# Order of loads, early offsets and one product for two sums ahead of the first tile of a two-layer graph kernel

## The chip, the cores and the metric

One core of a Trainium2 chip. The time is device microseconds of one execution, the median of several. Lower is better.

## The reference

Input `x` is 4096 x 128, `adj` a 4096 x 4096 matrix of zeros and ones. Layer 0 computes, with h = x W:

```
e     = leaky_relu((h @ a_src)[:, None] + (h @ a_dst)[None, :], 0.2)
valid = (adj > 0) & (h.sum(axis=1) != 0)[None, :]
att   = softmax(where(valid, e, -1e9)), zeroed where not valid or below 1e-4, times the row's number of valid edges
x     = layernorm(x + elu(h + att @ h))
```

Layer 1 takes scores = leaky_relu(x @ ks.T, 0.2), sets those without an edge to -9e15, and computes x = layernorm(x + softmax(scores) @ ks).

## The kernel before

The rows are cut into 32 tiles of 128. A tile's 128 x 4096 attention lies in SBUF with the row on the partition. For each tile, layer 0 adds a mask (one 128 x 4096 bf16 tile of adjacency, loaded by a DMA that GpSimd issues with a cast from int32) to the destination scores `d_all`, takes the row maximum, bends (leaky relu), raises to exp with the row's offset as bias, cuts small entries, transposes on TensorE in four chunks of 1024 columns (`turn0`), copies these to SBUF and multiplies with h (`sum0`). Layer 1 does the like with the keys. Each engine has its own queue, written out by hand; engines meet only through semaphores. In a slot `t` TensorE works on tile t in layer 0 and on tile t - 1 in layer 1.

PSUM holds `work`, three slots of two banks (1024 f32 columns each), used in turn by everything that is transposed or scored, and two more banks for sums.

The change lies ahead of slot 1. There the program does, in this order:

- SP loads x in four parts, then the keys (`k_first`, `k_rest`), then the first two x tiles. GpSimd loads adjacency tile 0 when x part 1 has landed, tile 1 when part 3 has, then the f16 keys (`k_parts`).
- TensorE transposes x (`turn_x`) into `xT`; two vectors from W and a give v_src, v_dst and v_one (W times ones). `make_d(c)` multiplies 512 columns of `xT` with v_one and with v_dst, each widened to 128 equal columns: bank 0 of a `work` slot then holds the row sums of h, bank 1 the destination scores, both repeated on all 128 partitions. It is done 8 times. `make_h(r)` computes h in six fills of `work`.
- ScalarE reads them: `find_sign(c)` writes the sign of the sums to `zero_cols` (bf16), `keep_d(c)` copies the scores to `d_all`. Among them stand `first_bend0(k)`, the leaky relu of quarter k of tile 0, and `keep_h`. Then `raise0(0, 0)` and `raise0(0, 1)`, exp of the two halves.
- VectorE builds mask 0 (`build_mask(0)`), then per quarter `zero_quarter` (sign 0 becomes a large negative number), the minimum with the mask (line 720) and the addition of `d_all` with its row maximum (line 724). `build_mask(1)` stands between quarters 1 and 2. After quarter 3 the four maxima are reduced to `top0` (line 768, it raises `masked0`), then the whole of tile 1 is masked (lines 619, 627), then `threshold0(0)` and `cut(0, 0)`, `cut(0, 1)` wait for the exps. `first_slot` follows: mask 2, `keep_k_low` (the rest of the f16 keys, line 752), minimum 2, the reduction `absent` (line 780, from which GpSimd counts edges), maximum 2, `residual0(0)` (line 646, it waits for `sum0` and for GpSimd's `coef0`), then the low parts of the keys `k_low_part(c)`.
- GpSimd computes the row offset of tiles 0 and 1 in three dependent 128x1 instructions (`offset0`: neg line 866, row 870, bias 873), and issues the loads of tiles 2 and 3 behind them, then `coefficient(0)` (lines 879 to 891: edges, z_sum, rz, gate, coef).
- TensorE goes on with `turn0(0, c)`, three chunks of `sum0`, `turn_k(0)`, `turn_k(1)`, the last chunk of `sum0`, `turn_k(2)`, `turn_k(3)` (its `work` slot waits for `k_low_part(0)`), `turn_q(0)` and the scores of tile 0 (`score`, lines 313 to 318). With score chunk 3 begins slot 1.

Of the kernel before, what the change touches and what calls it, by code (L numbers as in the profile page):

```python
# [5 lines left out]
P = 128  # L6
# [22 lines left out]
def graph_layers(nc, x, adj, W, a, ks, out):  # L29
# [5 lines left out]
    PER = CHUNK // P  # L35
    D_CHUNKS = N // BANK
    HALF = N // 2
# [8 lines left out]
    with ExitStack() as ctx:  # L46
# [42 lines left out]
        v_sb = sb("v_sb", [P, 3])  # L89
        v_dst_wide = sb("v_dst_wide", [P, P])  # L90
        v_one_wide = sb("v_one_wide", [P, P])
        first_s = sb("first_s", [P, 2])
# [62 lines left out]
        xT_ready, h_ready, kT_high, kT_low = sem("xT_ready"), sem("h_ready"), sem("kT_high"), sem("kT_low")  # L155
        sign_found, zero_found, d_ready, first_masked = sem("sign_found"), sem("zero_found"), sem("d_ready"), sem("first_masked")
        first_topped, first_bent, first_counted = sem("first_topped"), sem("first_bent"), sem("first_counted")
# [36 lines left out]

        X_AT, D_AT, H_AT = 0, CHUNKS, CHUNKS + D_CHUNKS
        H_PER = 6
# [7 lines left out]
        @block.sync  # L204
        def _(sp):
            x_blocks = x.rearrange("(b p) d -> p b d", p=P)
            for c in range(CHUNKS):
                part = slice(c * PER, (c + 1) * PER)
                sp.dma_start(x_all[:, part, :], x_blocks[:, part, :]).then_inc(xall_in[c], 16)
            k_blocks = ks.rearrange("(b p) d -> p b d", p=P)  # L210
            sp.dma_start(k_first, k_blocks[:, 0:SPLIT * PER, :]).then_inc(kall_in, 16)
            sp.dma_start(k_rest[:, :, 0:D], k_blocks[:, SPLIT * PER:BLOCKS, :]).then_inc(kall_in, 16)
            sp.dma_start(x_sb[0][:, :], x_rows[0]).then_inc(x_in[0], 16)
            sp.dma_start(x_sb[1][:, :], x_rows[1]).then_inc(x_in[1], 16)

            def slot(t):
                if t + 2 < TILES:
                    sp.wait_ge(low0_ready, t + 1)
                    sp.dma_start(x_sb[t % 2][:, :], x_rows[t + 2]).then_inc(x_in[t % 2], 16)
                if t >= 2:  # L220
                    w = t - 2
                    sp.wait_ge(x2_ready, w + 1)
                    sp.dma_start(out_rows[w], x2[w % 2][:, :]).then_inc(out_sent[w % 2], 16)

            for t in range(TILES + 2):
                slot(t)
            for p in range(2):
                sp.wait_ge(out_sent[p], 16 * (TILES // 2))

        @block.tensor  # L230
        def _(pe):
# [11 lines left out]
            def make_d(c):  # L243
                pe.wait_ge(xT_ready, c + 2 if c < 3 else CHUNKS)
                if c >= 3:
                    pe.wait_ge(d_ready, c - 2)
                    pe.wait_ge(sign_found, c - 2)
                rhs = xT[:, c * BANK:(c + 1) * BANK]
                place = (D_AT + c) % SLOTS
                pe.matmul(work[:, place, 0:BANK], v_one_wide[:, :], rhs, start=True, stop=True)  # L250
                pe.matmul(work[:, place, BANK:CHUNK], v_dst_wide[:, :], rhs, start=True, stop=True).then_inc(d_made, 1)

            def make_h(r):
                if r < 3:
                    pe.wait_ge(d_ready, r + 6)
                    pe.wait_ge(sign_found, r + 6)
                else:
                    pe.wait_ge(h_ready, r - 2)
# [6 lines left out]

            def turn_k(c):
                if c < 3:
# [20 lines left out]
            pe.wait_ge(wide_ready, 2)  # L288
            for c in range(D_CHUNKS):
                make_d(c)  # L290
            for r in range(H_FILLS):
                make_h(r)
            pe.wait_ge(kall_in, 32)

# [26 lines left out]
            def turn0(t, c):  # L321
# [3 lines left out]
                elif t > 0:  # L325
                    pe.wait_ge(bent1, 4 * (t - 1) + c + 2)
                else:
                    pe.wait_ge(h_ready, (5, 6, 4)[c])
                turn((1, 2, 0, 1)[c], c, lambda b: att0[t % 2][:, b * P:(b + 1) * P]).then_inc(turned0, 1)
# [97 lines left out]
        def _(act):  # L427
# [3 lines left out]
            for c in range(CHUNKS):  # L431
                act.wait_ge(x_turned, c + 1)
                nc.scalar.copy(xT[:, cols(c)], work[:, (X_AT + c) % SLOTS, :]).then_inc(xT_ready, 1)
            def find_sign(c):
                act.wait_ge(d_made, c + 1)
                nc.scalar.activation(zero_cols[:, c * BANK:(c + 1) * BANK], work[:, (D_AT + c) % SLOTS, 0:BANK],
                                     ACT.Sign).then_inc(sign_found, 1)

            def keep_d(c):
                act.wait_ge(d_made, c + 1)  # L440
                nc.scalar.copy(d_all[:, c * BANK:(c + 1) * BANK],
                               work[:, (D_AT + c) % SLOTS, BANK:CHUNK]).then_inc(d_ready, 1)

# [85 lines left out]
            def to_first_slot():  # L529
                find_sign(0)  # L530
                keep_d(0)
                find_sign(1)
                keep_d(1)
                find_sign(2)
                keep_d(2)
                find_sign(3)
                keep_d(3)
                first_bend0(0)
                find_sign(4)
                keep_d(4)  # L540
                find_sign(5)
                keep_d(5)
                first_bend0(1)
                find_sign(6)
                keep_d(6)
                find_sign(7)
                keep_d(7)
                keep_h(0)
# [60 lines left out]
        def _(dve):  # L609
# [106 lines left out]
            def first_mask0(k):  # L716
                both = adj_sb[0]
                dve.wait_ge(mask_built, 1)
                dve.wait_ge(zero_found, k + 1)
# [3 lines left out]
                dve.wait_ge(d_ready, (k + 1) * D_CHUNKS // QUARTERS)  # L723
# [4 lines left out]
            def zero_quarter(k):  # L728
                dve.wait_ge(sign_found, (k + 1) * D_CHUNKS // QUARTERS)
                z = zero_cols[:, quarter(k)]  # L730
                nc.vector.tensor_scalar(z, z, 0.0, -NO_EDGE, ALU.is_equal, ALU.mult).then_inc(zero_found, 1)

# [12 lines left out]
            dve.wait_ge(consts_ready, 2)  # L745
            nc.vector.tensor_scalar(v_dst_wide[:, :], ones[:, :], v_sb[:, 1:2], None, ALU.mult).then_inc(wide_ready, 1)
            nc.vector.tensor_scalar(v_one_wide[:, :], ones[:, :], v_sb[:, 2:3], None, ALU.mult).then_inc(wide_ready, 1)

# [5 lines left out]
            def to_first_slot():  # L754
                build_mask(0)
                zero_quarter(0)
                first_mask0(0)
                zero_quarter(1)
                dve.wait_ge(s_made, 1)
                nc.vector.tensor_copy(first_s[:, :], s_ps).then_inc(first_s_ready, 1)  # L760
                first_mask0(1)
                build_mask(1)
                zero_quarter(2)
                first_mask0(2)
                zero_quarter(3)
                first_mask0(3)
                dve.wait_ge(first_topped, QUARTERS)
                nc.vector.tensor_reduce(top0[0][:, :], first_top[:, :], AX.X, ALU.max).then_inc(masked0, 1)
                zero_mask(1)
                mask0(1)  # L770
                threshold0(0)
                cut(0, 0)
                cut(0, 1)

            def first_slot():
                build_mask(2)
                keep_k_low()
                zero_mask(2)
                dve.wait_ge(first_bent, QUARTERS)
                nc.vector.tensor_reduce(absent[0][:, :], first_absent[:, :], AX.X, ALU.add).then_inc(first_counted, 1)  # L780
                mask0(2)
# [60 lines left out]
        def _(pool):  # L842
# [16 lines left out]
            def offset0(f):  # L859
                p = f % 2  # L860
                pool.wait_ge(masked0, f + 1)
                if f < 2:
                    pool.wait_ge(first_s_ready, 1)
                else:
                    pool.wait_ge(s_ready, H_FILLS)
                nc.gpsimd.tensor_scalar(neg0[p][:, :], top0[p][:, :], -1.0, s_of(f), ALU.mult,  # L866
# [35 lines left out]
            def deviation1(w):  # L902
# [47 lines left out]
```

## Time and profile before

| what | value |
|---|---|
| median of 3 runs | 885.51 us (885.41 to 885.6) |
| the profiled execution: its time | 886.26 us |
| its span | 884.4 us |
| busy: PE, DVE, ACT, POOL | 849.4, 783.3, 763.8, 231.0 us |
| chain that ended last, by engine | PE 90%, DVE 3%, DMA 2%, POOL 2%, issue 2%, ACT 1% |
| PE busy, first four fortieths of the span (22 us each) | 7, 4, 7, 9 tenths |

### The profile page before, as it was taken

To read this page: it belongs to the slowest core of one execution; us is meant where nothing else is said; L and a number is where in the kernel's file an instruction comes from. 1 tells how busy PE (TensorE), PEld (TensorE's weight loads), DVE (VectorE), ACT (ScalarE), POOL (GpSimd) and SP (SyncE) were. 2 spreads that over 40 slices of the span, in tenths; PEclk is the share of its full clock that TensorE was granted. 3 is DMA by queue.
4 is the path that set the end of the run, shared out by engine and by line. 5 is a ranking of instruction groups with operands and counts; after the bars stand their busy time and mean duration, and the time that the engine had idled before them with its cause. 6 is when DMAs were issued, how large, how long until landed. Compare 5 with 4: busy or idle time off the path is not lost.

```text
span 884.4 us, 17581 instructions
## 1 busy us (share of the span) xinstructions
PE 849.4 (96%) x7111; PEld 732.9 (83%) x7111; DVE 783.3 (89%) x955; ACT 763.8 (86%) x747; POOL 231.0 (26%) x428
## 2 busy tenths in 40 slices
PE   7479999999999999999999999999999999999995
PEld 4376788899888888988888889888888998888885
DVE  1789999999999999999999999999999999998744
ACT  4588988889998888899988888999888889998753
POOL 1431143321223333212233331122333312222200
PEclk9898999999999999999999999999999999999999
DMA  9832222122222211222222112222221122200000
GB/s 236 124 67 50 52 49 41 28 43 55 54 55 54 55 34 30 47 54 55 54 54 54 28 32 53 54 55 54 55 52 24 34 55 54 55 7 7 4 4 10
DMA packets 23408, 43.93 MB, mean 50 GB/s; under 512 B 5024, under 2 KB 18464, under 8 KB 19232
## 3 DMA queue, kind: packets, MB, share of 16 engines
q0 software_dynamic: 7696, 34.34, 21.5%
q1 hardware_dynamic: 15200, 8.39, 3.7%
q8 instruction: 57, 0.93, 0.4%
q14 instruction: 23, 0.19, 0.1%
q10 hardware_dynamic: 432, 0.07, 0.1%
HBM read 75.04 MB, written 2.10 MB: 87 GB/s over the span
## 4 chain that ended last, share of the span: by engine, by line
PE 90%; DVE 3%; DMA 2%; POOL 2%; issue 2%; ACT 1%; POOLq 0%; SPq 0%; DVEq 0%; ACTq 0%
PE bank L336 25%; PE work L234 24%; PE bank L364 10%; PE bank L368 6%; PE work L313 6%; PE work L318 6%; PE work L314 6%; PE bank L365 5%; DMA adj_sb<-adj 1%; DMA att<-x 1%; POOL row L870 0%; POOL edges L879 0%; PE bank L374 0%; DVE att1T L690 0%; ACT att L460 0%
## 5 line engine op out<-in xcount | busy, mean ns | idle before, releaser
L234 PE MATMUL work<-ident,att 128*128 128x128 f32 x2080 | 245.9, 274 | 11.9 <-DMA att<-x 6.0
L234 PEld LDWEIGHTS work<-ident,att 128*128 128x128 f32 x2080 | 232.5, 141 | 19.3 <-issue 9.2
L336 PE MATMUL bank<-h_all,att0T 128*128 128x128 f32 x2048 | 239.1, 275 | 0.0
L336 PEld LDWEIGHTS bank<-h_all,att0T 128*128 128x128 f32 x2048 | 233.7, 192 | 0.0
L500 ACT ACTIVATE att1T<-work 128x1024 f16<-128x1024 f32 (+1 forms) x128 | 125.5, 1048 | 34.7 <-PE work L234 34.7
L640 DVE SCALAR_TENSOR_TENSOR att<-att,cut 128x2048 f32<-128x2048 f32 x64 | 149.7, 2343 | 0.0
L679 DVE CUSTOM_DVE_ANT_0 att<-att,mask 128x2048 f32<-128x2048 f32 x64 | 144.3, 2290 | 5.4 <-ACT att L483 5.4
L364 PE MATMUL bank<-k_parts,att1T 128*128 128x257 f16 x768 | 140.1, 275 | 0.8 <-DVE att1T L690 0.8
L627 DVE CUSTOM_DVE_ANT_0 att<-adj_sb,d_all 128x4096 f32<-128x4096 bf16 x31 | 137.2, 4425 | 1.0
L470 ACT ACTIVATE att<-att,bias 128x2048 f32<-128x2048 f32 x64 | 129.3, 2020 | 7.7 <-POOL bias L873 7.7
L365 PE MATMUL bank<-k_parts,att1T 128*128 128x129 f16 x768 | 134.9, 219 | 0.0
L488 ACT ACTIVATE att<-att,bias 128x2048 f32<-128x2048 f32 x64 | 131.9, 2062 | 2.7 <-DVE bias L685 2.7
L477 ACT COPY att0T<-work 128x1024 f32<-128x1024 f32 x128 | 129.4, 1049 | 1.5 <-PE work L234 1.5
L483 ACT ACTIVATE att<-work 128x1024 f32<-128x1024 f32 x128 | 121.6, 1027 | 8.8 <-PE work L318 8.8
L866 POOL TENSOR_SCALAR neg<-top,s_all 128x1 f32<-128x1 f32 x30 | 9.4, 314 | 425.6 <-DVE top L627 425.5
L690 DVE SCALAR_TENSOR_TENSOR att1T<-work,att1T 128x1024 f16<-128x1024 f32 x96 | 113.9, 1215 | 3.2 <-ACT att1T L500 3.2
L453 ACT ACTIVATE att<-att,s_all 128x4096 f32<-128x4096 f32 x30 | 111.4, 3712 | 0.0
L313 PE MATMUL work<-kT,qT 128*128 128x512 f16 x256 | 97.9, 383 | 0.9 <-ACT qT L510 0.9
L314 PE MATMUL work<-kT,qT 128*128 128x512 f16 x256 | 97.9, 383 | 0.0
L364 PEld LDWEIGHTS bank<-k_parts,att1T 128*128 128x128 f16 x768 | 74.2, 97 | 12.1 <-DVE att1T L690 1.0
L318 PE MATMUL work<-kT,qT 128*128 128x512 f16 x256 | 77.1, 383 | 0.0
L365 PEld LDWEIGHTS bank<-k_parts,att1T 128*128 128x128 f16 x768 | 75.8, 99 | 0.8
(98 smaller groups left out, 836.7 us busy)
## 6 DMA issues: line engine op xcount, KB each, us to landing
adj_sb<-adj POOLq DMA_DIRECT2D x32, 1024.0 KB, 8.6
att<-x SPq DMA_DIRECT2D x4, 512.0 KB, 6.6
x_sb<-x SPq DMA_DIRECT2D x32, 64.0 KB, 8.2
out<-x SPq DMA_DIRECT2D x32, 64.0 KB, 1.6
k_parts<-ks POOLq DMA_DIRECT2D x1, 768.0 KB, 20.6
k_rest<-ks SPq DMA_DIRECT2D x1, 512.0 KB, 21.9
w_sb<-W ACTq DMA_DIRECT2D x1, 64.0 KB, 2.9
a_sb<-a ACTq DMA_DIRECT2D x2, 0.5 KB, 4.8
```

What stands on the lines that cost most here:

```text
L234: mm = pe.transpose(work[:, n % SLOTS, b * P:(b + 1) * P], source(c * PER + b), ident[:, :])
L313: pe.matmul(o, qT[:, 0, :], kT[:, 0, part], start=True, stop=False)
L314: pe.matmul(o, qT[:, 0, :], kT[:, 1, part], start=False, stop=False)
L318: mm = pe.matmul(o, qT[:, 1, :], kT[:, 0, part], start=False, stop=True)
L336: mm = pe.matmul(acc0, att0T[:, k * P:(k + 1) * P], h_all[:, k, :], start=(k == 0), stop=(k == BLOCKS - 1))
L364: pe.matmul(acc1, high1T[:, part], k_parts[:, k, :], start=(k == 0), stop=False)
L365: mm = pe.matmul(acc1[:, D:], low1T[:, part], k_parts[:, k, D:], start=False, stop=(k == BLOCKS - 1))
L477: nc.scalar.copy(att0T[:, cols(c)], work[:, (1, 2, 0, 1)[c], :]).then_inc(copied0, 1)
L488: nc.scalar.activation(att1[:, half(k)], att1[:, half(k)], ACT.Exp, bias=bias1[u % 2][:, :]).then_inc(exp1, 1)
L627: nc.vector.tensor_tensor_reduce(att0[p][:, :], adj_sb[p][:, :], d_all[:, :], 1.0, -NO_ROW_MAX, ALU.add, ALU.max, top0[p][:, :]).then_inc( ...
L640: nc.vector.scalar_tensor_tensor(b, b, cut0[p][:, :], b, ALU.is_ge, ALU.mult).then_inc(cut_done, 1)
L679: nc.vector.tensor_tensor_reduce(att1[:, half(k)], att1[:, half(k)], mask[u % MASKS][:, half(k)], 1.0, -3.0e38, ALU.add, ALU.max, top1[u % ...
```

## The change

Loads: SP waits for adjacency tile 0 ahead of the key loads, GpSimd for tile 1 ahead of its own, and TensorE waits for the keys in `turn_k`.

Destination scores and zero sums: one widened matrix `v_wide` holds v_dst in columns 0 to 63 and v_one in columns 64 to 127, so one product gives the scores on partitions 0 to 63 and the sums on partitions 64 to 127. It is taken over 1024 columns at a time, four times. `keep_d(c)` copies the lower 64 partitions of PSUM twice, to either half of `d_all`. The sums of the second bank go through ScalarE's sign as before, but to each half by an instruction; those of the first bank are tested against zero by VectorE straight from PSUM, to each half by an instruction (`first_zero`). `second_zero` does for 512 columns what `zero_quarter` did for 1024.

Offsets: those of tiles 0 and 1 are computed on VectorE (`first_offset0`). `build_mask(1)` moves behind the offset of tile 0, and the `absent` reduction to a place ahead of the first threshold.

```diff
@@ sync
+            sp.wait_ge(adj_in[0], 16)
             sp.dma_start(k_first, k_blocks[:, 0:SPLIT * PER, :]).then_inc(kall_in, 16)
@@ tensor
             def make_d(c):
                 pe.wait_ge(xT_ready, c + 2 if c < 3 else CHUNKS)
-                if c >= 3:
-                    pe.wait_ge(d_ready, c - 2)
-                    pe.wait_ge(sign_found, c - 2)
-                rhs = xT[:, c * BANK:(c + 1) * BANK]
-                place = (D_AT + c) % SLOTS
-                pe.matmul(work[:, place, 0:BANK], v_one_wide[:, :], rhs, start=True, stop=True)
-                pe.matmul(work[:, place, BANK:CHUNK], v_dst_wide[:, :], rhs, start=True, stop=True).then_inc(d_made, 1)
+                if c == 3:
+                    pe.wait_ge(d_ready, 2)
+                    pe.wait_ge(sign_found, 2)
+                    pe.wait_ge(first_zero_found, 2)
+                for b in range(CHUNK // BANK):
+                    mm = pe.matmul(work[:, (D_AT + c) % SLOTS, b * BANK:(b + 1) * BANK], v_wide[:, :],
+                                   xT[:, c * CHUNK + b * BANK:c * CHUNK + (b + 1) * BANK], start=True, stop=True)
+                mm.then_inc(d_made, 1)
...
-                    pe.wait_ge(h_ready, (5, 6, 4)[c])
+                    pe.wait_ge(h_ready, (6, 4, 5)[c])
@@ scalar
             def keep_d(c):
                 act.wait_ge(d_made, c + 1)
-                nc.scalar.copy(d_all[:, c * BANK:(c + 1) * BANK],
-                               work[:, (D_AT + c) % SLOTS, BANK:CHUNK]).then_inc(d_ready, 1)
+                source = work[0:HP, (D_AT + c) % SLOTS, :]
+                nc.scalar.copy(d_all[0:HP, cols(c)], source).then_inc(d_ready, 1)
+                nc.scalar.copy(d_all[HP:P, cols(c)], source).then_inc(d_ready, 1)
+
+            def find_sign(c):
+
+                act.wait_ge(d_made, c + 1)
+                source = work[HP:P, (D_AT + c) % SLOTS, BANK:CHUNK]
+                for lower in range(0, P, HP):
+                    nc.scalar.activation(zero_cols[lower:lower + HP, c * CHUNK + BANK:(c + 1) * CHUNK], source,
+                                         ACT.Sign).then_inc(sign_found, 1)
...
                 find_sign(1)
                 keep_d(1)
+                first_bend0(0)
                 find_sign(2)
                 keep_d(2)
+                first_bend0(1)
                 find_sign(3)
                 keep_d(3)
...
                 keep_h(0)
                 first_bend0(2)
                 raise0(0, 0)
@@ vector
+            def first_zero(c):
+                dve.wait_ge(d_made, c + 1)
+                source = work[HP:P, (D_AT + c) % SLOTS, 0:BANK]
+                for lower in range(0, P, HP):
+                    nc.vector.tensor_scalar(zero_cols[lower:lower + HP, c * CHUNK:c * CHUNK + BANK], source, 0.0, -NO_EDGE,
+                                            ALU.is_equal, ALU.mult).then_inc(first_zero_found, 1)
+
+            def second_zero(c):
+                dve.wait_ge(sign_found, 2 * c + 2)
+                z = zero_cols[:, c * CHUNK + BANK:(c + 1) * CHUNK]
+                nc.vector.tensor_scalar(z, z, 0.0, -NO_EDGE, ALU.is_equal, ALU.mult).then_inc(second_zero_found, 1)
...
+            def first_offset0(f):
+                p = f % 2
+                dve.wait_ge(masked0, f + 1)
+                dve.wait_ge(first_s_ready, 1)
+                nc.vector.tensor_scalar(neg0[p][:, :], top0[p][:, :], -1.0, s_of(f), ALU.mult,
+                                        ALU.subtract).then_inc(neg0_ready, 1)
+
+                dve.wait_ge(neg0_ready, f + 1)
+                nc.vector.scalar_tensor_tensor(row0[p][:, :], neg0[p][:, :], NO_ROW_MAX / 2, neg0[p][:, :], ALU.is_lt,
+                                               ALU.mult).then_inc(row0_ready, 1)
+                dve.wait_ge(row0_ready, f + 1)
+                nc.vector.scalar_tensor_tensor(bias0[p][:, :], row0[p][:, :], SLOPE, row0[p][:, :], ALU.mult,
+                                               ALU.min).then_inc(bias0_ready, 1)
...
             def to_first_slot():
-                build_mask(0)
-                zero_quarter(0)
-                first_mask0(0)
-                zero_quarter(1)
+                first_zero(0)
                 dve.wait_ge(s_made, 1)
                 nc.vector.tensor_copy(first_s[:, :], s_ps).then_inc(first_s_ready, 1)
+                first_zero(1)
+                build_mask(0)
+                second_zero(0)
+                first_mask0(0)
+                first_zero(2)
+                second_zero(1)
                 first_mask0(1)
-                build_mask(1)
-                zero_quarter(2)
+                first_zero(3)
+                second_zero(2)
                 first_mask0(2)
-                zero_quarter(3)
+                second_zero(3)
                 first_mask0(3)
                 dve.wait_ge(first_topped, QUARTERS)
                 nc.vector.tensor_reduce(top0[0][:, :], first_top[:, :], AX.X, ALU.max).then_inc(masked0, 1)
+                first_offset0(0)
+                build_mask(1)
                 zero_mask(1)
                 mask0(1)
+                first_offset0(1)
+                dve.wait_ge(first_bent, QUARTERS)
+                nc.vector.tensor_reduce(absent[0][:, :], first_absent[:, :], AX.X, ALU.add).then_inc(first_counted, 1)
                 threshold0(0)
@@ gpsimd
+            pool.wait_ge(adj_in[1], 16)
             pool.wait_ge(k_one_ready, 2)
             nc.gpsimd.dma_start(k_parts[:, :, D:2 * D],
                                 ks.rearrange("(b p) d -> p b d", p=P)[:, 0:SPLIT * PER, :]).then_inc(k_high, 16)
-            offset0(0)
             load_adj(2)
-            offset0(1)
             load_adj(3)
             coefficient(0)
```

The slots of `make_h` and their waits are renumbered to the four products.

## Rows read from the trace of the kernel before

**Rows 1.** Chain of waits, whole span: start us, us, what.

```profile
101.30 3.49 PE work L234 x32
...
836.82 3.49 PE work L234 x32
```

**Rows 2.** Chain of waits, first 80 us.

```profile
7.87 11.33 DMA adj_sb<-adj
19.23 1.23 DVE mask L614
...
31.98 2.28 POOL neg L866
...
56.83 4.34 POOL edges L879
...
63.10 0.36 DVE y L646
```

**Rows 3.** Timeline, 0 to 45 us: start us, us, instruction, idle time before it.

```profile
14.22 0.60 ACT L436 ACTIVATE zero_cols<-work 128x512 bf16<-128x512 f32 x1 [1.15 <-PE work L251]
...
15.94 0.60 ACT L436 ACTIVATE zero_cols<-work 128x512 bf16<-128x512 f32 x1 [0.64 <-PE work L251]
...
31.77 2.28 DVE L619 TENSOR_TENSOR adj_sb<-mask,zero_cols 128x4096 bf16<-128x4096 bf16 x1
...
34.09 4.42 DVE L627 CUSTOM_DVE_ANT_0 att<-adj_sb,d_all 128x4096 f32<-128x4096 bf16 x1
```

**Rows 4.** All instructions of line 870: ns least, median, most; first and last start.

```profile
L870 POOL TENSOR_SCALAR row<-neg x32: 310/311/4337, 34.4 to 798.5; 128x1 f32<-128x1 f32 x32
```

**Rows 5.** Adjacency tile, first 110 us: from issue to landing.

```profile
DMA to landing us min/median/max: 8.5/10.0/13.7
```

**Rows 6.** Groups by shape, first 80 us: count, busy us, mean ns, idle us before.

```profile
L724 DVE CUSTOM_DVE_ANT_0 att<-adj_sb,d_all 128x1024 f32<-128x1024 bf16 x4 | 4.9, 1225 | 0.1
L735 DVE TENSOR_TENSOR kT<-work,kT 128x1024 f16<-128x1024 f32 x4 | 4.8, 1208 | 0.0
L436 ACT ACTIVATE zero_cols<-work 128x512 bf16<-128x512 f32 x8 | 4.8, 603 | 3.1 <-PE work L251 3.1
...
L433 ACT COPY att<-work 128x1024 f32<-128x1024 f32 x4 | 4.1, 1013 | 5.6 <-PE work L234 5.6
...
L720 DVE TENSOR_TENSOR adj_sb<-mask,zero_cols 128x1024 bf16<-128x1024 bf16 x4 | 2.8, 692 | 0.3
L731 DVE TENSOR_SCALAR zero_cols<-zero_cols 128x1024 bf16<-128x1024 bf16 x4 | 1.7, 422 | 0.4 <-ACT zero_cols L436 0.4
...
L633 DVE TENSOR_SCALAR cut<-z 128x1 f32<-128x1 f32 x2 | 0.4, 210 | 6.7 <-ACT att L470 6.7
```

**Rows 7.** Timeline, 43 to 69 us.

```profile
43.22 2.09 PE L262 MATMUL work<-w_sb,att 128*128 128x129 f32 x8 [10.24 <-ACT h_all L523]
...
45.44 4.62 DVE L640 SCALAR_TENSOR_TENSOR att<-att,cut 128x2048 f32<-128x2048 f32 x2
...
47.89 1.94 PE L234 MATMUL work<-ident,att 128*128 128x128 f32 x16 [0.85 <-DVE att L640]
...
59.02 1.95 PE L336 MATMUL bank<-h_all,att0T 128*128 128x128 f32 x16
...
60.89 0.99 ACT L527 CAST kT<-work 128x1024 f16<-128x1024 f32 x1
...
68.83 0.58 PE L313 MATMUL work<-kT,qT 128*128 128x512 f16 x1 [0.90 <-ACT qT L510]
```

**Rows 8.** Stretches of 1 us: busy time by engine, granted clock, DMA share, GB/s.

```profile
46.00:47.00 1.00, 1.00 (x5) 0.85 (x4) 1.00 (x1) 1.00 (x3) 0.00 (x0) 0.62 0.91 188
67.00:68.00 1.00, 0.48 (x1) 0.18 (x1) 1.00 (x3) 0.20 (x2) 0.73 (x4) 0.62 0.00 0
74.00:75.00 1.00, 1.00 (x6) 0.44 (x5) 0.38 (x1) 0.86 (x1) 0.00 (x0) 0.97 1.17 246
175.00:176.00 1.00, 1.00 (x7) 0.46 (x5) 1.00 (x1) 1.00 (x2) 0.00 (x0) 1.00 1.04 156
```

More of the change, by code:

```diff
@@ L35, in graph_layers @@
     PER = CHUNK // P
-    D_CHUNKS = N // BANK
+    HP = P // 2
     HALF = N // 2
@@ L89, in graph_layers @@
         v_sb = sb("v_sb", [P, 3])
-        v_dst_wide = sb("v_dst_wide", [P, P])
-        v_one_wide = sb("v_one_wide", [P, P])
+        v_wide = sb("v_wide", [P, P])
         first_s = sb("first_s", [P, 2])
@@ L155, in graph_layers @@
         xT_ready, h_ready, kT_high, kT_low = sem("xT_ready"), sem("h_ready"), sem("kT_high"), sem("kT_low")
-        sign_found, zero_found, d_ready, first_masked = sem("sign_found"), sem("zero_found"), sem("d_ready"), sem("first_masked")
+        sign_found, first_zero_found, second_zero_found, d_ready, first_masked = (
+            sem("sign_found"), sem("first_zero_found"), sem("second_zero_found"), sem("d_ready"), sem("first_masked"))
         first_topped, first_bent, first_counted = sem("first_topped"), sem("first_bent"), sem("first_counted")
@@ L191, in quarter @@
             return slice(k * QUARTER, (k + 1) * QUARTER)
-        X_AT, D_AT, H_AT = 0, CHUNKS, CHUNKS + D_CHUNKS
+        X_AT, D_AT, H_AT = 0, CHUNKS, 2 * CHUNKS
         H_PER = 6
@@ L244, in make_d @@
                 pe.wait_ge(xT_ready, c + 2 if c < 3 else CHUNKS)
-                if c >= 3:
-                    pe.wait_ge(d_ready, c - 2)
-                    pe.wait_ge(sign_found, c - 2)
-                rhs = xT[:, c * BANK:(c + 1) * BANK]
-                place = (D_AT + c) % SLOTS
-                pe.matmul(work[:, place, 0:BANK], v_one_wide[:, :], rhs, start=True, stop=True)
-                pe.matmul(work[:, place, BANK:CHUNK], v_dst_wide[:, :], rhs, start=True, stop=True).then_inc(d_made, 1)
+                if c == 3:
[6 more added lines that the diff above has]
+                mm.then_inc(d_made, 1)
             def make_h(r):
                 if r < 3:
-                    pe.wait_ge(d_ready, r + 6)
-                    pe.wait_ge(sign_found, r + 6)
+                    pe.wait_ge(d_ready, 2 * r + 4)
+                    pe.wait_ge(sign_found, 2 * r + 4)
+                    pe.wait_ge(first_zero_found, 2 * r + 4)
                 else:
@@ L266, in turn_k @@
             def turn_k(c):
+                pe.wait_ge(kall_in, 32)
                 if c < 3:
@@ L288, in _ @@
             pe.wait_ge(wide_ready, 2)
-            for c in range(D_CHUNKS):
+            for c in range(CHUNKS):
                 make_d(c)
@@ L292, in _ @@
                 make_h(r)
-            pe.wait_ge(kall_in, 32)
             def score(t, c):
@@ L433, in _, with keep_d @@
                 nc.scalar.copy(xT[:, cols(c)], work[:, (X_AT + c) % SLOTS, :]).then_inc(xT_ready, 1)
+            def keep_d(c):
+                act.wait_ge(d_made, c + 1)
+                source = work[0:HP, (D_AT + c) % SLOTS, :]
+                nc.scalar.copy(d_all[0:HP, cols(c)], source).then_inc(d_ready, 1)
+                nc.scalar.copy(d_all[HP:P, cols(c)], source).then_inc(d_ready, 1)
             def find_sign(c):
                 act.wait_ge(d_made, c + 1)
[L436 to L440, printed above, removed]
-                nc.scalar.copy(d_all[:, c * BANK:(c + 1) * BANK],
-                               work[:, (D_AT + c) % SLOTS, BANK:CHUNK]).then_inc(d_ready, 1)
+                source = work[HP:P, (D_AT + c) % SLOTS, BANK:CHUNK]
+                for lower in range(0, P, HP):
+                    nc.scalar.activation(zero_cols[lower:lower + HP, c * CHUNK + BANK:(c + 1) * CHUNK], source,
+                                         ACT.Sign).then_inc(sign_found, 1)
             def bend0(f):
@@ L533, in to_first_slot @@
                 keep_d(1)
+                first_bend0(0)
                 find_sign(2)
                 keep_d(2)
+                first_bend0(1)
                 find_sign(3)
                 keep_d(3)
[L538 to L547, printed above, removed]
                 keep_h(0)
@@ L718, in first_mask0 @@
                 dve.wait_ge(mask_built, 1)
-                dve.wait_ge(zero_found, k + 1)
+                dve.wait_ge(first_zero_found, 2 * k + 2)
+                dve.wait_ge(second_zero_found, k + 1)
                 nc.vector.tensor_tensor(both[:, quarter(k)], mask[0][:, quarter(k)], zero_cols[:, quarter(k)],
@@ L722, in first_mask0 @@
                 dve.wait_ge(first_masked, k + 1)
-                dve.wait_ge(d_ready, (k + 1) * D_CHUNKS // QUARTERS)
+                dve.wait_ge(d_ready, 2 * k + 2)
                 nc.vector.tensor_tensor_reduce(att0[0][:, quarter(k)], both[:, quarter(k)], d_all[:, quarter(k)],
@@ L726, in first_mask0 @@
                                                first_top[:, k:k + 1]).then_inc(first_topped, 1)
[L728 to L731, printed above, removed]
+            def first_zero(c):
[8 more added lines that the diff above has]
+                nc.vector.tensor_scalar(z, z, 0.0, -NO_EDGE, ALU.is_equal, ALU.mult).then_inc(second_zero_found, 1)
             def k_low_part(c):
@@ L745, in _ @@
             dve.wait_ge(consts_ready, 2)
-            nc.vector.tensor_scalar(v_dst_wide[:, :], ones[:, :], v_sb[:, 1:2], None, ALU.mult).then_inc(wide_ready, 1)
-            nc.vector.tensor_scalar(v_one_wide[:, :], ones[:, :], v_sb[:, 2:3], None, ALU.mult).then_inc(wide_ready, 1)
+            nc.vector.tensor_scalar(v_wide[:, 0:HP], ones[:, 0:HP], v_sb[:, 1:2], None, ALU.mult).then_inc(wide_ready, 1)
+            nc.vector.tensor_scalar(v_wide[:, HP:P], ones[:, HP:P], v_sb[:, 2:3], None, ALU.mult).then_inc(wide_ready, 1)
+            def first_offset0(f):
[10 more added lines that the diff above has]
+                                               ALU.min).then_inc(bias0_ready, 1)
             def keep_k_low():
@@ L778, in first_slot @@
                 zero_mask(2)
-                dve.wait_ge(first_bent, QUARTERS)
-                nc.vector.tensor_reduce(absent[0][:, :], first_absent[:, :], AX.X, ALU.add).then_inc(first_counted, 1)
                 mask0(2)
@@ L861, in offset0 @@
                 pool.wait_ge(masked0, f + 1)
[L862 to L865, printed above, removed]
+                pool.wait_ge(s_ready, H_FILLS)
                 nc.gpsimd.tensor_scalar(neg0[p][:, :], top0[p][:, :], -1.0, s_of(f), ALU.mult,
```

## The prediction

> **What bounds the kernel now.** I read the chain of waits first. From the first full slot to the last but one the same entry (32 transposes) returns from 101.30 to 836.82 us, 29 slots of 25.36 us, always on TensorE [rows 1]. The diff changes no instruction of these slots but two branches of a helper, so what it can move is the start of slot 1, before which the chain runs over other engines [rows 2]: the landing of adjacency tile 0 (19.2 us), the mask work on VectorE, GpSimd's offset (31.98 to 39.1), its edge count (56.83) and the residual it holds up (63.10). The timeline then says what stood beside each. GpSimd's `row` took 4.34 us once and 0.31 in its other 31 runs, and that once it lies inside VectorE's 4.42 us mask instruction, `neg` inside the 2.28 us one before it [rows 2 to 4]. The edge count, 4.34 us too, starts 0.1 us behind the same 4.42 us instruction of tile 2. So some 6 us of the offset and 4 of the edge count are a wait for VectorE, not work.
>
> **Keys behind the adjacency.** SP now issues the two key loads when tile 0 has landed, GpSimd its own behind tile 1. `x_sb` follows the keys on SP. GpSimd's load 2 no longer stands behind offset 0: issued at 30.3 (below), it lands 8.5 to 10 later, by 40, and is read at 44.65. Tile 0 took 11.33 us; the shortest landing of an adjacency tile is 8.5 [rows 2, 5]. It still shares with the last two x loads, so I take 16.4 to 18.4 us, middle 17.4 instead of 19.2. Keys and tile 1 must land by 45.8 and 30.9 (below). Before, all this traffic was over by 32 us, and its bytes are the same. I cost it at nothing.
>
> **One product per 1024 columns.** TensorE did 16 products of 512 columns, now 8. Product c of the new kernel occupies the time of one old pair: ready at 14.2, 15.9, 17.7, 19.4 the first two are 1.72 apart [rows 3]. The readers change. ScalarE did 2 signs and 2 copies of 512 per 1024 columns, at a pitch of 0.48 each (the next starts before one of 0.60 has ended), 1.9 us; now 2 signs of 512 and 2 copies of 1024 on 64 partitions. The trace has no 64-partition form. The bounds are half of the 128-partition copy (1.01 for 1024 columns [rows 6]) and twice it; I take it whole, pitch 0.93. That is 2.8 us per 1024 columns, 3.7 more in all. VectorE gets 8 reads of 64x512 from PSUM: bounds 0.42 (the 1024-column SBUF form) and 1.21 (1024 columns with a PSUM operand), I take half the latter, 0.60, so 1.2 per 1024 columns; its remaining zero pass halves (0.42 to about 0.3, pitch with the semaphore 0.4) [rows 6].
>
> The new front, by queue. VectorE: `first_zero(0)` 14.2 to 15.4, scores copy, `first_zero(1)` 15.95 to 17.15; mask 0 at 17.4, 1.15; then 0.4 + 0.72 + 1.15 per quarter (zero, minimum, maximum) and 1.2 for each `first_zero`: quarter 0 done 20.8, quarter 1 at 24.3, quarter 2 at 27.7. ScalarE: sign(0), keep(0), sign(1), keep(1) to 19.9; waits for quarter 0; bend 20.9 to 22.0; sign(2), keep(2) to 24.8; bend, sign(3), keep(3) to 28.7. The last maximum waits for that keep: 28.8 to 30.0. So the two engines bind about equally, tile 0's 0.25 us included, and the row maximum is ready at 30.2, before at 31.86: 1.7 earlier.
>
> **Offset on VectorE.** Three 128x1 instructions, 0.21 each by the `cut` threshold's row [rows 6], with semaphores 0.25: 0.75 in all (bounds 0.3 and 1.1). The bias is ready at 30.95 instead of 39.1. ScalarE: exp half 0 from 31.0, bend(3), `keep_h(1)`, exp half 1 done at 36.9, before 45.1 (the threshold, 0.21, stands between it and the cut at 45.44): 8.2 earlier. But VectorE is late next. Mask 1 was built ahead of quarter 2, where VectorE waited for signs; now it stands behind the offset: 1.15, then minimum and maximum of tile 1 (6.75, from 31.77 to 38.5 [rows 3]), offset 1 (0.75) and the moved `absent` reduction (0.2): the threshold can't start before 39.8, `cut` at 40.05, before at 45.44 [rows 7]. Gain at this point 5.4, not 8.2; 1.9 of it is build and offset that lost their cover.
>
> **TensorE's clock takes some back.** Before, h fills ran from 43.2 on right ahead of the transposes at 47.89; the engine had idled 10.2 us, the granted clock was 0.5 (1.2 GHz) and rose at about 46.8 (0.62 is the mean of that microsecond) [rows 7, 8]. Now the fills end at 38.6 and the transposes start at 42.45 behind idle time, so at 1.2 GHz. It rose 3.5 us after work began there and 5.2 after the scores began (68.83 to 74.1) [rows 7, 8]. Transposes at half speed for 3.5 to 5.2 us lose 1.75 to 2.6, less the 0.45 that TensorE waited for the second cut anyway; taken 1.7. The four transposed chunks and the sum then end at 60.97 - 5.4 + 1.7 = 57.2 [rows 7].
>
> **Edge count moved forward.** It starts at 39.8 beside the cuts. If each of its five GpSimd instructions waits for one VectorE instruction it is done at 51.4 (cuts, mask 2, key part, minimum 2), before 57.2: nothing on the path. VectorE: cuts to 44.65, mask 2, key part, minimum, maximum of tile 2 as before, ending at 61.1 (where the blocked edge count came free [rows 2]) - 5.4 - 0.1 = 55.6. So the residual waits for TensorE at 57.3 in place of GpSimd at 63.10 [rows 2]: 5.8 earlier. The first key copy on ScalarE stands behind the transposed copies, 60.89 - 5.4 + 1.7 = 57.2, done 58.1, and doesn't hold that up by more than 0.1. From there to the scores all is as before, 68.83 - 5.75 = 63.1. Offset 2 stays on GpSimd behind mask 2 and coefficient 0, both done.
>
> The scores ran at 1.2 GHz for 5.2 us before, losing 2.6; the clock had fallen at 67.2, in a stretch (61 to 68.8) with little work [rows 8]. With the 2 us wait for GpSimd gone this stretch is 2 us shorter. Either the same again (0) or no fall (+2.6, of which VectorE's masks let through about 1.8); I add 0.6. **Sum: 5.75 + 0.6 = 6.35 us off the profiled execution**, 886.26 (span 884.4 and 1.86 around it) to 879.9. The median of runs is 0.75 below the profiled one, so 879.2.
>
> **Rivals.**
> (a) Clock kept through the scores: 1.8 instead of 0.6 and a loss of 0.8 instead of 1.7 at 42.45: 5.75 + 0.9 + 1.8 = 8.45, so 877.1. For it: shorter gaps. Against: the clock fell in the same place before.
> (b) Tile 0 lands no sooner, 19.2: the front moves 1.8 us later, gain 4.5: 881.0. For it: x loads still share; against: 2 MB of keys leave its way.
> (c) Adjacency tile 2 is held up: its issue is now followed by back-to-back VectorE work to 38.6, and GpSimd stood still beside such work [rows 3, 4]. Held to 38.6 it lands at 47.1 to 48.6 instead of 40, mask 2 waits from 44.65, maximum 2 ends at 58.1 to 59.6, 0.9 to 2.4 behind TensorE: about 880.8. Against: in the slot of 174 us a load was moving at 175 with VectorE busy throughout [rows 8]. A rule speaks for it: while VectorE runs an instruction in a two-port mode, GpSimd cannot write the descriptors of a DMA that it issues (the Trainium skill, "SBUF — State Buffer", section "SBUF: two separate sides"). By its wording only the mask build here is of that kind, which makes the landing 1.2 later and the sum no different, 879.2; if it held for all of VectorE's forms in the stretch, it would be the 880.8 above. The row at 175 agrees with the narrow reading.
> (d) Slower: 64-partition instructions (8 copies, 8 signs, 8 PSUM reads) that read one half and write the other cost double. ScalarE's front grows by 4 x (1.86 + 0.96) = 11.3 us, of which about 1 falls into its waits. The cut then starts 10.3 later: 885.5 - 6.3 + 10.3 = 889.5. It decides at an extra of about 60% an instruction, where the gain is gone. For it: no row of the form. Against: full-width rows go by columns.
> (e) The offset on VectorE brings nothing because mask 1 moved behind it: the cut at 45.4. Against: the sum above leaves VectorE no such length. What is left is the edge count's 2.0 less the clock's part: about 884.5.
>
> **Chances.** Forecast 0.50 (own range 878 to 880.5), (a) 0.20, (b) 0.12, (c) 0.08, (d) 0.06, (e) 0.04. The range 876.5 to 883.5 leaves out (d), (e) and the tails of the rest, under 0.2: its low end is (a) with half-width copies somewhat under 1 us, its high end (b) and (c) together and 0.9 more for dearer half-width forms. Within 0.2% is 1.8 us, about what can be told from no change here. Faster by more: all but (d) and (e), 0.90; within: (e), 0.04; slower: (d), 0.06.
>
> **What would show it.** Tile 0's mask starts near 17.4. The first two `row` and `neg` are VectorE's, near 30.5. Exp half 1 ends near 37 and the cut starts near 40, with VectorE and not ScalarE as the last. Transposes from 42.4 at a granted 0.5. The residual at 57.3, released by TensorE. Scores from 63.1. Slots still 25.36 apart, 101.30 now near 95. Wrong: a 64-partition copy far from 1.0 us; a cut after 42; a residual still released by GpSimd; slots of another length.

## The result and the profile after

The changed kernel takes 882.15 us (median of 5, 880.22 to 882.62), the kernel before 885.51 in the same session; the ratio is 0.9956, 95% interval 0.9941 to 0.9971. It is faster by 3.9 us with 2.6 to 5.2 as the interval (3.4 by the medians), where 6.3 was forecast. Two of its five runs took 880.2 and 880.5 us and three 882.2 to 882.6; its profiled execution is the longest of them, 882.62 us with a span of 880.7. In one experiment below, `e6_offset_pool`, one run of eleven took 1113.8 us at a mean granted clock of 0.749 (0.981 to 0.989 in the others) and is left out of its numbers.

The chain of waits of the changed kernel, against [rows 1]:

```profile
97.57 3.49 PE work L238 x32
...
833.07 3.49 PE work L238 x32
```

Again 29 slots of 25.36 us, all 3.73 earlier. So the whole gain stands ahead of slot 1, as forecast. Its timeline there, in order of time (start us, us, instruction, idle time before it and what ended it):

```profile
14.45 1.21 ACT L451 ACTIVATE zero_cols<-work 64x512 bf16<-64x512 f32 x2 [1.15 <-PE work L254]
14.45 1.42 DVE L735 TENSOR_SCALAR zero_cols<-work 64x512 bf16<-64x512 f32 x2 [4.28 <-PE work L254]
15.68 1.00 ACT L443 COPY d_all<-work 64x1024 f32<-64x1024 f32 x1
...
16.71 1.00 ACT L444 COPY d_all<-work 64x1024 f32<-64x1024 f32 x1
17.07 0.83 SPq L215 DMA_DIRECT2D att1T<-ks  x1
17.61 1.23 DVE L616 TENSOR_SCALAR mask<-adj_sb 128x4096 bf16<-128x4096 bf16 x1
17.74 1.21 ACT L451 ACTIVATE zero_cols<-work 64x512 bf16<-64x512 f32 x2
...
30.40 1.23 DVE L727 CUSTOM_DVE_ANT_0 att<-adj_sb,d_all 128x1024 f32<-128x1024 bf16 x1 [0.74 <-ACT d_all L444]
...
31.86 0.21 DVE L763 TENSOR_SCALAR neg<-top,first_s 128x1 f32<-128x1 f32 x1
...
32.56 2.01 ACT L480 ACTIVATE att<-att,bias 128x2048 f32<-128x2048 f32 x1 [0.28 <-DVE bias L770]
...
36.43 2.01 ACT L480 ACTIVATE att<-att,bias 128x2048 f32<-128x2048 f32 x1
...
41.34 4.63 DVE L642 SCALAR_TENSOR_TENSOR att<-att,cut 128x2048 f32<-128x2048 f32 x2
...
43.76 6.60 PE L238 MATMUL work<-ident,att 128*128 128x128 f32 x32 [3.66 <-DVE att L642]
...
52.79 4.42 POOL L918 TENSOR_SCALAR coef<-gate,rz 128x1 f32<-128x1 f32 x1
...
59.36 0.35 DVE L648 SCALAR_TENSOR_TENSOR y<-bank,coef,h_all 128x128 f32<-128x128 f32 x1 [2.31 <-PE bank L342]
...
65.23 0.58 PE L319 MATMUL work<-kT,qT 128*128 128x512 f16 x1 [0.90 <-ACT qT L520]
```

What to see in it: SP's wait for tile 0 ends at 17.07, the mask build stands at 17.61 right behind `first_zero(1)` with no wait of its own (19.23 before [rows 2]). The row maximum is reduced at 31.67 (31.70 before), so this front gained nothing, and the offset starts right behind it at 31.86. The bias is there at 32.5 instead of 39.1. VectorE runs on without a wait to the cut at 41.34 (45.44 before), while the exps were done at 38.4. The residual is at 59.36 and waits for TensorE, no longer for GpSimd at 63.10; GpSimd's last instruction for it (`coef`) ended at 57.21. The 32 transposes take 6.6 us; before, the two lots of 16 took 1.94 and 1.97 with a gap of 0.28. The granted clock is the third number from the end of each row below (a row gives the stretch and its length, the busy time of PE, PEld, which is TensorE's loading of weights, DVE, ACT and POOL, then the clock, the DMA share and GB/s):

```profile
42.00:43.00 1.00, 0.00 (x0) 0.00 (x0) 1.00 (x1) 0.00 (x0) 1.00 (x1) 0.94 1.42 131
43.00:44.00 1.00, 0.24 (x1) 0.24 (x2) 1.00 (x2) 0.00 (x0) 0.92 (x2) 0.50 0.71 139
49.00:50.00 1.00, 1.00 (x8) 1.00 (x7) 1.00 (x1) 0.82 (x1) 1.00 (x1) 0.64 0.00 0
63.00:64.00 1.00, 0.14 (x1) 0.14 (x1) 1.00 (x3) 0.63 (x1) 0.81 (x3) 0.68 0.00 0
70.00:71.00 1.00, 1.00 (x6) 0.42 (x5) 0.79 (x1) 0.54 (x1) 0.00 (x0) 0.90 0.99 197
```

The mean of a microsecond tells when the clock changed within it. It fell to 0.50 (1.2 GHz) at 42.9, in 3.7 us of idleness behind the h fills and just ahead of the transposes, and came back at about 49.7; it fell once more at 63.3, ahead of the scores, until 70.2.

### The profile page after: what moved, and what is told of

The parts are those of the page before. It is cut to its first block, busy times and chain, and to the rows that moved or that the text cites. A ratio compares the mean times of both kernels' runs of the same rounds, so it can differ in the third digit from the quotient of the medians.

```text
span 880.7 us, 17559 instructions
## 1 busy us (share of the span) xinstructions
PE 846.5 (96%) x7095; PEld 733.3 (83%) x7095; DVE 789.0 (90%) x969; ACT 768.3 (87%) x747; POOL 231.6 (26%) x422
## 4 chain that ended last, share of the span: by engine, by line
PE 92%; DVE 3%; ACT 2%; issue 2%; DMA 1%; SPq 0%; POOL 0%; POOLq 0%; DVEq 0%; ACTq 0%
PE work L238 25%; PE bank L342 25%; PE bank L370 10%; PE bank L374 6%; PE work L319 6%; PE work L320 6%; PE work L324 6%; PE bank L371 5%; DMA att<-x 1%; PE bank L380 0%; ACT att L463 0%; DVE att1T L692 0%; PE work L254 0%; SPq L212 0%; DVE mask L616 0%
## 5 line engine op out<-in xcount | busy, mean ns | idle before, releaser
L238 PEld LDWEIGHTS work<-ident,att 128*128 128x128 f32 x2080 | 235.0, 143 | 22.3 <-issue 8.6
L370 PEld LDWEIGHTS bank<-k_parts,att1T 128*128 128x128 f16 x768 | 74.2, 97 | 12.0 <-DVE att1T L692 1.0
L918 POOL TENSOR_SCALAR coef<-gate,rz 128x1 f32<-128x1 f32 x32 | 78.0, 2438 | 3.3
```

The source lines that it names most:

```text
L238: mm = pe.transpose(work[:, n % SLOTS, b * P:(b + 1) * P], source(c * PER + b), ident[:, :])
L370: pe.matmul(acc1, high1T[:, part], k_parts[:, k, :], start=(k == 0), stop=False)
```

## Experiments

Each kernel is compared with the kernel before in its own session (885.6 to 886.6); the ratios carry that, the medians differ by up to 1 us between sessions. "Changed" is the changed kernel. The diffs shown here are abridged. The clock's part varies from trace to trace, and there is one trace of each kernel: the 32 transposes took from 4.2 us (before) to 6.6 (changed).

**The product.** `e1_no_product` takes it out of the changed kernel, `e2_product_only` puts it alone into the kernel before.

```diff
@@ e1_no_product, against changed
-pe.matmul(work[:, place, b * BANK:...], v_wide, xT[:, ...])                    # 8
+pe.matmul(work[:, place, 0:BANK], v_one_wide, rhs); pe.matmul(..., v_dst_wide, rhs)  # 16
-first_zero(c), second_zero(c), find_sign(c), keep_d(c)   # half-width, on 1024 columns
+find_sign(c), keep_d(c)   # 128x512, for each of 8 products
+zero_quarter(k)
```

> The changed kernel with the 16 full-width products, 8 signs, 8 copies and zero_quarter of the kernel before in place of the half-width product; loads, VectorE offsets and the earlier edge count stay. Theory P (the half-width forms cost what the saved product work was worth, and more): the row maximum of tile 0 is ready by about 30.3 us instead of 31.8, and the time is 1 to 1.5 below the changed kernel, about 881. Rival (the product brought its share of the 3.4 us): the row maximum comes later than 31.8 and the time is 883.5 or more.

> The kernel before with the half-width product, signs, copies and first_zero alone; keys first, offsets on GpSimd, edge count late, mask 1 between quarters 1 and 2 as before. Theory P: no gain, 885.5 to 887, the row maximum at 31.8 to 33.5. Rival (the product brings a share by itself): 884 or less.

Without the product 878.91 us, ratio 0.9920 (0.9907 to 0.9932), against 0.9956 with it: 3.2 us faster. With the product alone 887.92, ratio 1.0026 (1.0017 to 1.0036): 2.3 us slower than before, and a little above the 885.5 to 887 expected; its row maximum is reduced at 33.96 instead of 31.70. VectorE in `e1_no_product`:

```profile
16.34 1.23 DVE L615 TENSOR_SCALAR mask<-adj_sb 128x4096 bf16<-128x4096 bf16 x1 [6.11 <-DMA adj_sb<-adj]
...
23.21 0.43 DVE L732 TENSOR_SCALAR zero_cols<-zero_cols 128x1024 bf16<-128x1024 bf16 x1 [0.85 <-ACT zero_cols L437]
...
29.17 0.16 DVE L782 TENSOR_REDUCE top<-first_top 128x1 f32<-128x4 f32 x1
...
38.84 4.64 DVE L641 SCALAR_TENSOR_TENSOR att<-att,cut 128x2048 f32<-128x2048 f32 x2
```

The row maximum is ready 2.5 us earlier than with the product (31.67) and so is the cut. VectorE now waits 6.11 us for tile 0 and 0.85 for a sign; with the product it didn't wait for tile 0, and waited 0.74 for ScalarE's last copy. Theory P holds, and by more than the 1 to 1.5 expected. Part of the 3.2 us is the clock's: the 32 transposes took 5.28 us here and 6.60 in the changed kernel.

**What a half-width instruction costs.** `e7_halves` doubles the score copies of the kernel before in two ways (one run, 888.28 us).

```diff
-nc.scalar.copy(d_all[:, ...], source)
+nc.scalar.copy(to[0:64], source[0:64]); nc.scalar.copy(to[64:128], source[64:128])   # c < 4
+nc.scalar.copy(to, source); nc.scalar.copy(unused, source)                           # c >= 4
```

> The kernel before with two ways to copy the destination scores twice: for products 0 to 3 the lower and the upper 64 partitions by an instruction each, partition onto the same partition; for products 4 to 7 all 128 partitions twice, the second time to unused memory. It measures the pitch of ScalarE's instructions. Theory H (64 partitions lose the overlap with the next instruction): pitch of a 64-partition copy of 512 columns 0.58 to 0.62, of a 128-partition one 0.48. Rival (the crossing to the other half costs it): here, where nothing crosses, both have 0.48. Second rival (two reads of the same PSUM columns in a row lose it): both have 0.6. The time says nothing else.

```profile
15.01 0.57 ACT L444 COPY d_all<-work 64x512 f32<-64x512 f32 x1
15.59 0.58 ACT L445 COPY d_all<-work 64x512 f32<-64x512 f32 x1
16.24 0.60 ACT L437 ACTIVATE zero_cols<-work 128x512 bf16<-128x512 f32 x1
...
25.11 0.58 ACT L447 COPY d_all<-work 128x512 f32<-128x512 f32 x1
25.58 0.60 ACT L448 COPY kT<-work 128x512 f32<-128x512 f32 x1
26.06 0.63 ACT L437 ACTIVATE zero_cols<-work 128x512 bf16<-128x512 f32 x1
```

The duration is the same, 0.57 on 64 partitions and 0.58 on 128, but behind a half-width copy the next instruction starts 0.58 us later (15.01 to 15.59), behind a full one 0.47 (25.11 to 25.58, 25.58 to 26.06). Nothing crosses to other partitions here, and the full-width copy read the same columns twice in a row: both rivals fall, theory H holds. In the changed kernel the copies of 1024 are 1.03 apart (15.68, 16.71, 17.74), the signs 0.6.

**The key loads.** `e5_keys_early` undoes them in the changed kernel, `e10_keys_only` does them alone in the kernel before (the three waits on `adj_in` and `kall_in`).

> The changed kernel with the key loads issued as before, ahead of the adjacency. Theory L (the later key loads bring tile 0's mask forward by what lies between its landing and first_zero(1)): tile 0's mask starts at 19.4 to 19.5 instead of 17.6, the row maximum at about 33.5 instead of 31.8, the time 1.5 to 1.9 higher than the changed kernel, about 883.8. Rival (ScalarE's reads bind the front, tile 0's landing is hidden): row maximum within 0.3 of 31.8, 882.1.

> The kernel before with the later key loads alone. Theory L: tile 0's mask starts at 16.4 instead of 19.2, but ScalarE's signs and copies bind the last quarter, so the row maximum is ready at about 30.3 instead of 31.9 and all that follows moves by that: 884, 1.5 below before. Rival: the later keys or the moved f16 load cost something of their own and it is 885.5 or more.

Undone: 882.99 us, ratio 0.9969 (0.9957 to 0.9981), 1.1 by ratio over the changed kernel, whose intervals overlap; in its trace tile 0's mask starts at 19.27 and the row maximum is reduced at 33.33 instead of 31.67. Alone: 883.85, ratio 0.9974 (0.9962 to 0.9985), 2.3 faster than before, with the mask at 16.40 and the maximum at 29.24, 2.5 ahead of before and 1 ahead of what I expected. Theory L holds in the traces and, alone, in the time; undone, the time moved by less than the 1.5 to 1.9 expected, which by itself would show nothing.

**The offset.** `e6_offset_pool` puts the two offsets back on GpSimd; `e11_offset_only` has them on VectorE, with the earlier edge count, as the only edits of the kernel before.

> The changed kernel with the offsets of tiles 0 and 1 back on GpSimd, all else as changed (mask 1 still behind the row maximum, edge count ahead of the threshold). Theory O (GpSimd's three 128x1 instructions wait for VectorE's mask work, one each): neg, row and bias end at about 40.5, exp half 1 at 46.5, the cut at 46.7 instead of 41.3 and later than the kernel before's 45.4, the time 885 to 887. Rival (only part of the wait is real, since the mask 1 build lets neg through): cut below 44, time below 884.

> The kernel before with VectorE's offsets and the earlier edge count alone, mask 1 built between quarters 1 and 2 as before. Theory O: the cut starts at 40.5 instead of 45.4, the residual about 2 us further forward less the low clock's part, time 880.5 to 881.5. Rival (the gain needs the earlier tile 0 too): 883 or more.

`e6_offset_pool`: 885.1 us, ratio 0.9991 (0.9982 to 1.0), 3.1 slower than changed by ratio, with the cut at 45.87 instead of 41.34. All three of GpSimd's 128x1 instructions now take the time of VectorE's instruction beside them:

```profile
31.35 1.22 DVE L616 TENSOR_SCALAR mask<-adj_sb 128x4096 bf16<-128x4096 bf16 x1
31.56 1.20 POOL L894 TENSOR_SCALAR neg<-top,first_s 128x1 f32<-128x1 f32 x1 [8.06 <-DVE top L795]
32.86 2.21 POOL L898 TENSOR_SCALAR row<-neg 128x1 f32<-128x1 f32 x1
35.16 4.37 POOL L901 TENSOR_SCALAR bias<-row 128x1 f32<-128x1 f32 x1
...
40.11 0.31 POOL L894 TENSOR_SCALAR neg<-top,first_s 128x1 f32<-128x1 f32 x1
```

`bias` was the short one in the kernel before; here it stands beside the row-maximum instruction and takes 4.37. So it is the neighbour that makes the time, not the operation. `e11_offset_only`: 879.91 us, ratio 0.9929 (0.9916 to 0.9941), 6.3 faster than before, cut at 39.99; both are somewhat better than expected, and the rival falls. It is by far the largest part of the change, and by itself it is 2.4 us faster than the whole change. No run has the earlier edge count alone, so the 6.3 is of the two together.

**TensorE's clock.** `e3_warm_first` adds 28 transposes into unused PSUM ahead of the first real ones, `e3b_warm_both` another 25 in the gaps ahead of the scores.

```diff
+def idle_work(n):
+    for _ in range(n): pe.transpose(wT_ps, w_sb[:, 0:D], ident[:, :])
+idle_work(28)            # both
 turn0(0, 0) ...
 turn_k(2)
+idle_work(10)            # e3b_warm_both only; 9 behind turn_k(3), 6 behind turn_q(0)
```

> The changed kernel with 28 transposes that nobody reads behind the h fills, ahead of turn0(0, 0). Theory C (the low clock at the first transposes takes 2.4 us back): granted clock 1.00 at 44 us, 32 transposes in about 4.2 us instead of 6.6, time 2 us lower, about 880, and runs closer together. Rival (VectorE's masks of tile 2 end at 57 anyway and bind next): the transposes are faster but the residual starts less than 0.5 us earlier and the time stays 882.

> As e3_warm_first, with 10, 9 and 6 more transposes that nobody reads behind turn_k(2), turn_k(3) and turn_q(0). Theory C: the granted clock stays 1.00 through the first scores, which take 3.9 us instead of 6.5; VectorE's masks then bind in slot 1, and the time is 1 to 2 below e3_warm_first's 879.5, about 878. Rival: VectorE's chain takes it all, 879.5; or the added transposes themselves delay the key transposes and it is above 879.5.

```profile
43.00:44.00 1.00, 0.34 (x3) 0.24 (x3) 1.00 (x2) 0.00 (x0) 0.92 (x2) 1.00 0.80 156
```

`e3_warm_first` (the row above is its own): clock 1.00, the cut and the first transpose at the same 41.35 and 43.76, the 32 transposes in 4.2 us, the residual at 57.25 instead of 59.36, 879.53 us, ratio 0.9931 (0.9919 to 0.9944): 2.2 by ratio, 2.6 by medians; the five runs lie within 1.1 us, those of the changed kernel within 2.4. TensorE's sum was done at 56.89. The residual then waited for GpSimd, whose `coef` took the time of VectorE's row-maximum instruction on tile 2 (done at 57.05):

```profile
52.79 4.42 POOL L923 TENSOR_SCALAR coef<-gate,rz 128x1 f32<-128x1 f32 x1
...
57.25 0.35 DVE L653 SCALAR_TENSOR_TENSOR y<-bank,coef,h_all 128x128 f32<-128x128 f32 x1 [0.19 <-POOL coef L923]
```

`e3b_warm_both`: granted clock 1.00 in every microsecond I read from 60 to 67, 878.12 us, ratio 0.9914 (0.9900 to 0.9927). Both clock losses are real, 2.2 and about 1.4 us, though the intervals of the two kernels overlap a little. In `e3_warm_first` the scores ran at 0.50 for 2.8 us (62.98 to 65.8), not for 5.0 as in the changed kernel; half of 2.8 is the 1.4.

**VectorE's order.** `e4_cut_first` moves tile 1's maximum and offset behind the cuts, the f16 key rest ahead of the threshold, coefficient 0 ahead of load 3.

> The changed kernel with the masks of tile 1's maximum (4.4 us) and its offset moved behind the cuts of tile 0, the f16 key rest (3.3 us) moved ahead of the threshold, and coefficient 0 ahead of load 3 on GpSimd. Theory V (VectorE's tile 1 work holds the cut, not ScalarE's exps): the cut starts at 39.6 instead of 41.3, ScalarE's exp half 1 (38.5) being next, and the time is 1.5 lower, about 880.6. Rival (the residual is bound by VectorE's work in all, which is the same): within 0.5 of 882.1.

879.50 us, ratio 0.9929 (0.9916 to 0.9941): the cut at 39.40, the residual at 56.98 right behind VectorE's mask of tile 2. It gained 2.4 where 1.5 was expected. The idle time ahead of the transposes shrank to 1.88 us and these took 5.24 instead of 6.60: a share of the gain is the clock's.

**All together.** `e8_all` has the full-width products, the order of `e4_cut_first` and 12, 10, 9 and 6 added transposes; `e9_no_product_cut_first` lacks the transposes.

> The full-width products of e1_no_product, the order of e4_cut_first, and transposes that nobody reads in the two gaps (12, then 10, 9 and 6). If the three effects stand beside each other: residual at about 54.6 (VectorE's masks of tile 2 next), scores at 2.4 GHz, time about 876.5. If VectorE already took all: 878.9, as e1_no_product.

> As e8_all without the added transposes. Theory V: the residual moves from 55.5 (e1_no_product) to 54.6, bound by VectorE, so 878 or 0.9 below e1_no_product's 878.9. Rival (TensorE's clock at the first transposes decides again): 878.9 or more.

`e8_all`: 875.92 us, ratio 0.9886 (0.9873 to 0.9900), 6.2 us below the changed kernel by ratio and the fastest of all. Its residual is at 56.40 and not at 54.6: TensorE's sum was done at 54.46, and VectorE's mask of tile 2 ended just at 56.40. Its cut came at 38.93, no earlier than the 38.84 of `e1_no_product`: with this order VectorE reads the f16 keys ahead of the cut, and it waited for them, since their load had been moved behind tile 1. It waited 1.43 us here and 0.84 in `e9_no_product_cut_first`; in the kernel before this load had landed at about 32:

```profile
35.41 3.36 DVE L775 TENSOR_TENSOR k_parts<-att1T,k_parts 128x3072 f16<-128x3072 f32 x1 [1.43 <-DMA k_parts<-ks]
```

So the later key load, which costs nothing in the changed kernel, costs something in this order. `e9_no_product_cut_first`: 878.61 us, ratio 0.9911 (0.9897 to 0.9924), not to be told from `e1_no_product`. Its cut came 0.6 earlier (38.25), its transposes took 6.50 us, and the residual stood at 56.17, behind `e1_no_product`'s 55.5: the rival, with one trace of each.

## Why the prediction was right, and where not

**Direction and place** were right: all of the gain is ahead of slot 1, 101.30 became 97.57, and the slots kept their 25.36 us. The size was 6.35 in the profiled execution, it is 3.64. The 882.15 us lie in the stated range (876.5 to 883.5) but not in the forecast's own (878 to 880.5). That the range held is in part luck: its high end was worked out from rivals (b) and (c), which didn't come, with 0.9 for dearer half-width forms, and what brought the time near that end is those forms and the clock. Three terms of the sum are off.

**The half-width product (row maximum 1.7 earlier: it was 0).** This is the term that failed most. I took a copy of 1024 on 64 partitions at a pitch of 0.93, a sign at 0.48 and a PSUM read at 0.60; they measured 1.03, 0.60 and 0.71. ScalarE needs 3.3 us for 1024 columns instead of 2.8, VectorE 3.75 for a quarter (28.55 - 24.80, from one quarter's end to the next) instead of 3.5. Both queues are full, ScalarE's to the end (VectorE waits 0.74 us for its last copy), so it adds up to 1.4 at the row maximum; 0.2 more is that the products began at 14.45 instead of 14.22. The nearest row was the right duration and the wrong pitch. And I forecast the sum of two edits as one number: the product costs 2.5 us at that place (`e1_no_product`), the key loads bring 2.5 (`e10_keys_only`), so the 1.7 hid a loss. Rival (d) had the sign of this one edit right, with an extra of about 17% on ScalarE (3.3 against 2.8), not 100%.

**The offset and its sequel (the cut 5.4 earlier: 4.1)** were right as a mechanism: GpSimd's 6 us were a wait for VectorE, they went, and VectorE's work on tile 1 was late next. What is missing is the front's loss, 1.6; from the row maximum to the cut the forecast was 9.85 us (30.2 to 40.05) and it took 9.5 (31.83 to 41.34).

**The clock (1.7 lost: 2.4)** was right in place. I didn't follow it through the h fills. It was at 0.50 from 36.1 on, came up at 39.5 during them, and fell again at 42.9, less than 1 us ahead of the transposes. So the transposes ran slow for 6.0 us instead of my 3.5 to 5.2. For the scores I added 0.6 and 0.1 came: they ran at 0.50 for 5.0 us instead of 5.2.

**Edge count and residual** were right in what releases the residual: TensorE's sum, done at 59.25, and not GpSimd. The time of GpSimd's last instruction was not: 51.4 forecast, 57.21 measured. I had given each of the five one VectorE instruction to wait for. The first, `edges`, waited for none (0.19 us). The next two took 2.21 and 3.19 us beside the two cuts and the mask build, `gate` 5.42 beside the f16 key rest and the minimum, and `coef` 4.42 beside the row maximum. So only 2.0 us were left before it would have held the residual again, and in `e3_warm_first` it did.

**Rivals.** (a) is not what happened; `e3b_warm_both` shows what it would have been, 878 (877.1 forecast). (b) did not come: tile 0 had landed by 17.07. (c) did not come: mask 2 was built right behind the cuts, at 45.90. (e) is refuted by the changed kernel itself: mask 1 stands behind the offset there, and the cut is at 41.34, not at 45.4; with the offset back on GpSimd (`e6_offset_pool`) it is at 45.87 and the time 3.1 us higher. `e11_offset_only` says nothing of (e), since it leaves mask 1 where it was. The edits by themselves, as ratios: offset and edge count 6.3 us, key loads 2.3, product -2.3. They don't add up to the 3.9 of the whole, since mask 1 stands behind the offset in the changed kernel and the clock's loss changes. The traces show both: from `e11_offset_only` to the changed kernel the row maximum is reduced at the same time (31.66 and 31.67), but the cut starts 1.35 us later and the transposes take 6.60 us instead of 5.35.

## What to carry to other kernels

Price each edit by itself even where two feed the same event: a gain and a loss of 2.5 us met here in one number near 0. A tiny GpSimd instruction on the critical path took as long here as the VectorE instruction beside it, or as two in a row; put it on the engine that produces its input. Halving TensorE's work in front of two reading engines that are full is worth nothing if it makes them read more often, and a gap that is opened ahead of TensorE can be paid twice, as it was in the changed kernel: once as idle time and once as the clock of the work behind it.

## What the runs showed of the hardware

- ScalarE started the next instruction 0.1 us before a 128-partition copy of 512 columns ended, and not before a 64-partition one ended (pitch 0.47 and 0.58, duration 0.58 and 0.57, in `e7_halves`); whether the copy crosses to the other half makes no difference that the rows show (the next starts 1.03 us behind either of the two copies of 1024 in the changed kernel).
- GpSimd's 128x1 instructions of 0.31 us lasted 1.20, 2.21 and 4.37 us beside VectorE's mask build, minimum and row-maximum instructions (`e6_offset_pool`), and `gate`, 0.32 elsewhere, 5.42 beside two in a row (changed kernel). The Trainium skill ("GPSIMD Engine Reference", section "8. Key points") has this contention for VectorE instructions in a two-port mode or with two SBUF inputs, and the rows agree for the minimum and the row maximum, which have two SBUF inputs. The mask build has one, and it held GpSimd up too; whether it runs in a two-port mode no row shows.
- In `e3_warm_first` 28 added transposes (3.2 us) ahead of the first real ones gave back 2.2 us: the granted clock was 1.00 in the microsecond that had 0.50 without them.
